# Row gathers with a growing lead, and batch 0's gathers back set among the last of them, in a routed-expert and linear-attention kernel

## The reference

```
x = x + 0.5 * ffn(layernorm(x))         # first expert stage
x = x + attn(layernorm(x))              # attention, then lookup network
x = x + 0.5 * ffn(layernorm(x))         # second expert stage

ffn(x):  probs = softmax(x @ router_W + router_b);  top1 = argmax(probs)
         h = relu(x @ W1[e] + b1[e])    # 128 -> 512, for each expert e
         y = h @ W2[e] + b2[e]          # 512 -> 128
         out = y of the expert top1, times its probability
attn(x): h = layernorm(x, g1, b1);  q, k, v = h @ wq, h @ wk, h @ wv;  16 heads of 8
         phi = elu + 1;  out = (phi(q) @ (phi(k)^T v)) / (phi(q) @ sum phi(k)) @ wo
         x = x + out;  x = x + table(layernorm(x, g2, b2) @ w1) @ w2
```

## Time and profile before

| | us |
|---|---|
| median of 3 runs | 212.8 (212.19 to 212.83) |
| profiled execution | 214.1 |
| its span | 212.4 |
| PE busy | 189.6 (89%) |
| DVE busy | 121.5 (57%) |
| POOL busy | 121.6 (57%) |
| ACT busy | 112.4 (53%) |
| mean granted TensorE clock | 0.947 of full |

### The profile page before, as it was taken

How to read it: one execution, slowest core, us unless ns; L and a number is a source line. 1 busy time by engine, 2 the same in 40 slices (tenths; PEclk the granted TensorE clock), 3 DMA queues, 4 the chain that set the end, 5 groups by cost and what they waited for, 6 DMA issues and landing times.

```text
span 212.4 us, 4556 instructions
## 1 busy us (share of the span) xinstructions
PE 189.6 (89%) x1416; PEld 159.7 (75%) x1416; DVE 121.5 (57%) x516; ACT 112.4 (53%) x328; POOL 121.6 (57%) x183
## 2 busy tenths in 40 slices
PE   4987969999997399889999999998997899999992
PEld 2963349999996398767876578688643899999991
DVE  4868312222221547889897946757531677777762
ACT  2666026555664066779869875131300766667670
POOL 6887664554467725653499704557673154455544
PEclk9965599999999679999999999999999999999998
DMA  6999959899683212059997000001028838776700
GB/s 182 256 380 346 327 166 325 266 273 305 195 297 98 73 39 77 26 204 415 420 415 315 3 2 3 27 27 44 27 74 274 279 127 296 237 258 220 260 27 0
DMA packets 26680, 40.26 MB, mean 190 GB/s; under 512 B 4229, under 2 KB 16296, under 8 KB 25632
## 3 DMA queue, kind: packets, MB, share of 16 engines
q1 hardware_dynamic: 21136, 33.01, 44.3%
q0 software_dynamic: 2496, 4.76, 7.4%
q10 hardware_dynamic: 3024, 2.20, 3.4%
HBM read 10.78 MB, written 14.46 MB: 119 GB/s over the span
## 4 chain that ended last, share of the span: by engine, by line
PE 61%; DVE 13%; issue 8%; POOL 7%; DMA 5%; ACT 4%; another core or an unknown queue 1%; POOLq 0%; DVEq 0%
PE bank L1076 19%; PE bank L1093 18%; PE bank L1213 6%; PE bank L1229 5%; PE bank L1069 2%; DMA xn_scratch<-xn 2%; DMA Xg<-xn_scratch,srcu 2%; DVE stat L1298 2%; ACT hT L726 2%; POOL xn L571 1%; PE bank L1168 1%; PE bank L1154 1%; PE bank L1178 1%; DVE phiq L1568 1%; DVE x L1531 1%
## 5 line engine op out<-in xcount | busy, mean ns | idle before, releaser
L726 ACT ACTIVATE hT<-bank,ewc_own 128x128 f32<-128x128 f32 x184 | 52.5, 368 | 50.1 <-PE bank L1076 48.7
L1076 PE MATMUL bank<-xT,ewc_own 128*128 128x128 f32 x368 | 50.3, 281 | 7.5 <-issue 5.6
L1076 PEld LDWEIGHTS bank<-xT,ewc_own 128*128 128x128 f32 x368 | 46.1, 197 | 8.7 <-issue 8.7
L1093 PE MATMUL bank<-ew,hT 128*128 x368 | 49.8, 279 | 0.5 <-ACT hT L726 0.5
L1093 PEld LDWEIGHTS bank<-ew,hT 128*128 128x128 f32 x368 | 45.6, 195 | 1.1 <-issue 1.1
L661 POOL DMA_INDIRECT out_dram<-ysb,eqrq x23 | 22.6, 983 | 26.6 <-issue 16.4
L594 POOL DMA_INDIRECT Xg<-xn_scratch,srcu x23 | 22.0, 957 | 19.2 <-PE bank L1069 15.7
L907 PE MATMUL bank<-ones_bf 128*128 128x512 bf16 x72 | 23.0, 455 | 3.1 <-POOL ident L489 2.7
L1435 DVE TENSOR_TENSOR ysb<-bank,ewc_own 128x128 f32<-128x128 f32 x23 | 6.7, 291 | 30.0 <-PE bank L1093 28.6
L653 POOL DMA_INDIRECT row_scratch<-pay,posu x16 | 15.8, 987 | 10.8 <-DVE posu L1402 6.8
L614 POOL DMA_INDIRECT xnT<-slot_scratch,posu x16 | 15.8, 988 | 10.3 <-DVE ysb L1435 4.6
(11 more groups left out here) (241 smaller groups left out, 302.2 us busy)
## 6 DMA issues: line engine op xcount, KB each, us to landing
ewc_own<-ew SPq DMA_DIRECT2D x46, 322.0 KB
row_scratch<-xn SPq DMA_DIRECT2D x8, 1024.0 KB, 10.6
ew<-in_L_ffn_W_dram SPq DMA_DIRECT2D x1, 2048.0 KB, 12.2
slot_scratch<-ysb SPq DMA_DIRECT2D x23, 64.0 KB
ew<-in_L_ffn_W_dram SPq DMA_DIRECT2D x5, 256.0 KB
eqrq<-row_scratch SPq DMA_DIRECT2D x18, 70.0 KB, 2.1
x<-in_L_attn_x_dram SPq DMA_DIRECT2D x4, 256.0 KB, 3.4
xn_scratch<-xn ACTq DMA_DIRECT2D x4, 256.0 KB, 5.8
```

Of the source, the lines that this page charges most:

```text
L726: last = A(hT[:, t.slot, c * P:(c + 1) * P], up_bank(k, c)[:, c * P:(c + 1) * P], ACT.Relu, scale=0.5 if m else 1.0, bias=ewc[t.ahead][:, ...
L1076: last = mm(up_bank(k, c)[:, c * P:(c + 1) * P], ewc[t.ahead][:, c * P:(c + 1) * P], xT[:, t.slot, :], start=True, stop=True)
L1093: last = mm(bank[4 + t.parity][:, 0:D], hT[:, t.slot, c * P:(c + 1) * P], ew[:, bass.ds(e[k], 1), W2_AT + c * D:W2_AT + (c + 1) * D].squee ...
```

## The change

`GATHERED = 4` stays the number of gathers that wait for nothing. After them the lead of the gathers over the transposes grows by one in every `GATHER_STEP = 3` gathers, up to the ring's 8 buffers (`turned_before`). From gather 21 on (`BACK_AMONG`) each gather has one of batch 0's gathers back ahead of it; the other two of batch 0 follow. The fill now stands behind the gathers back of batch 1.

```
-GATHERED = 4
+GATHERED, GATHER_STEP, BACK_AMONG = 4, 3, 21
...
+            def turned_before(k):
+
+                return k + 1 - min(UNROLL, GATHERED + (k - GATHERED) // GATHER_STEP)
+
             def move_rows():
 
                 def gather(k):
                     if k >= GATHERED:
-                        pool.wait_ge(xg_T, k - GATHERED + 1)
+                        pool.wait_ge(xg_T, turned_before(k))
...
                 for k in range(NT):
+                    if k == BACK_AMONG:
+                        pool.wait_ge(posu_ready, 1)
+                    if k >= BACK_AMONG:
+                        bring_back(0, k - BACK_AMONG)
                     gather(k)
-                g.memset(xn[:, :, :], 1.0).then_inc(fill_ready, 1)
-                pool.wait_ge(posu_ready, 1)
...
+            def bring_back(group, j):
+
+                t = group * GT + j
+                if j == 0:
+                    pool.wait_ge(y_stored[group], 16 * tiles_of(group))
+                if group + 1 < NG:
+                    pool.wait_ge(y_ready, min(NT - 1, UPTO[group] + 1 + j))
+                g.indirect_dma_start(out=Yg[:, t, :], out_offset=None, in_=slot_scr[0:UPTO[group] * P, :],
+                                     in_offset=bass.IndirectOffsetOnAxis(ap=posu[:, t:t + 1], axis=0)
+                                     ).then_inc(yb_in[group], 16)
...
             move_rows()
             for b in range(B):
-                bring_back(b)
+                for j in range(NT - BACK_AMONG if b == 0 else 0, GT):
+                    bring_back(b, j)
+                if b == 1:
+                    g.memset(xn[:, :, :], 1.0).then_inc(fill_ready, 1)
```

## The result

The changed kernel took 210.3 us, the median of 12 runs (208.67 to 212.06); the kernel before beside it took 212.91 (212.18 to 214.49, 12 runs). The ratio is 0.9873, 95% interval 0.9845 to 0.9901: faster by 2.7 us, where 6.0 were forecast and 206.8 us was the predicted time. It lies outside the range of 205.5 to 209.0.

What follows compares the result with a forecast made beforehand. PE's 5.26 us stall, from DVE's wait for batch 0's gathers back, was taken as the bound. Last down 6.4 us earlier, less 0.4 for the landing, gave 212.8 - 6.0 = 206.8 us; 8-in-10 range 205.5 to 209.0.

Steps and rivals of the forecast that it cites:

- What bounds the kernel: First expert stage: PE stalls 5.26 us before up(20), as DVE waits for batch 0's gathers back; slow matmuls follow.
- Lead of the row gathers: POOL's row gathers pull ahead, gather 20 going at about 50.7 instead of 58.2; cost and gain by itself 0.
- no wait for rows: PE did not wait for gathered rows before 67.4, busy 32.4 of 32.4 us, so the lead alone gives nothing.
- First gather back at 57.5: POOL starts batch 0's first gather back at 57.5, once the store of tile 10, issued at 54.70, has landed.
- rival A: Batch 0's data still come late: 208.8 us with the store landing late, 211.1 with back 3 late too; chance 0.12.
- Back 3 lands 2.52 us after its start on a quiet DMA: Batch 0's fourth gather back, started at 63.7, lands at 66.5 with 0.3 us added, leaving PE a 0.5 us hole.
- The fill beside DVE: The moved fill runs beside take_back and finish_rstd; POOL gives way and DVE loses at most 0.2 us.
- The sum: Last down 6.4 us earlier, less 0.4 lost to the landing: 6.0 us gained, 206.8 us forecast.
- The rest of the chain: Batch 0's statistics, guess at 69.60, normal1(0) at 71.1, then 3.84 us to the last down at 74.9, 6.4 earlier.
- B: The fill blocks DVE at the shared port during batch 0's statistics, taking 1.82 us of the gain: 208.6 us, chance 0.06.
- C: Slower: gathers 21 and 22 stand in POOL's list behind the wait for tile 10's store; 214.8 us, chance 0.03.
- D: Nothing changes, PE's hole at 67.44 having another reason than DVE's wait: 212.8 us, chance 0.04.

Runs made afterwards that it cites:

- r1: The changed kernel run again without an edit: 209.06 us beside 212.16 for the kernel before, ratio 0.9778.
- r3: The changed kernel run again without an edit, a third time: 209.8 us beside 212.97 for the kernel before, ratio 0.9885.
- r2: The changed kernel run again without an edit, a second time: 210.77 us beside 213.09 for the kernel before, ratio 0.9878.
- (2): The changed kernel with the row gathers' lead kept at 4: 0.9932 of the kernel before on a faster chip, 1.0013 and 1.0042 on slower ones.
- (4): The changed kernel with row gathers 21 and 22, then the fill, ahead of all gathers back: 206.55 of 212.16 us, 0.9726; slower chip 0.9957.
- (5): The kernel before with only the fill moved behind batch 1's gathers back: 212.52 of 212.16 us, 0.998.
- (6): The changed kernel with the fill cut into eight memsets at the same place: 209.94 of 213.09 us, 0.985; slower chip 1.0248.
- (7): (4) with ten attention weight loads moved from SP's turns 8 to 17 into its last five: 207.04 of 212.16 us, 0.9752.
- (8): (4) with weight loads of tiles 19 to 22 cut to a quarter of their columns: 206.0 of 213.09 us, 0.9668; slower chip 0.9997.
- (1): The changed kernel with the fill ahead of the wait for batch 0's first gather back: 220.26 of 216.92 us on a slower chip, 1.0127.

## Why the prediction was wrong

The steps compare best when each trace is measured from its own moment at which DVE has finished take_y(17) (start of take_back less its wait); that takes out how early or late the kernel's front ran. Us, faster chips only; "issue" is the fourth gather back's start after that moment (minus: before it), "landing" from its start to take_back, "rest" from that moment to the start of the last down:

| | issue | landing | DVE's wait | avar | rest |
|---|---|---|---|---|---|
| before; again | 2.9; 2.9 | 2.5; 2.5 | 5.5; 5.4 | 0.40; 0.17 | 15.6; 15.4 |
| forecast | -2.1 | 2.8 | 0.7 | 0.2 | 9.5 |
| changed, first trace | -0.5 | 4.3 | 3.7 | 1.70 | 15.0 |
| changed, r1; r3 | -1.7; -2.1 | 4.2; 4.4 | 2.5; 2.4 | 1.70 | 12.4; 12.4 |
| changed, r2 | -0.8 | 3.7 | 2.9 | 1.69 | 14.2 |
| (2) lead 4 | 0.0 | 2.6 | 2.5 | 2.21 | 13.0 |
| (4) rows first, fill in gap | -2.7 | 5.0 | 2.4 | 0.17 | 10.9 |
| (5) fill moved alone | 1.3 | 2.5 | 3.8 | 2.25 | 14.3 |
| (6) fill in pieces | -0.9 | 4.6 | 3.7 | 1.97 | 13.9 |
| (7) SP on time | -4.6 | 6.7 | 2.0 | 0.17 | 10.5 |
| (8) small last weights | -3.2 | at most 3.2 | 0 | 0.17 | 9.0 |

Step by step:

*What bounds the kernel* was right: PE's hole of 5.26 us shrank when the gathers back came earlier, to 3.51, 2.25, 2.71 and 2.14 in the four traces.

*Lead of the row gathers* and *no wait for rows*: gather 20 at 50.66 was forecast for 50.7, and PE stayed busy for all of 35 to 67.4 us. The cost of 0 that I took for the lead is not settled: its gain over a lead of 4 is 0.9885 against 0.9932 with overlapping intervals on one faster chip, and on the slower chips the kernels with the growing lead have the holes.

*First gather back at 57.5*: 58.98 in the first trace, where SP issued the store of tile 10 at 56.50 in place of 54.70, behind other loads and stores on its list; the landing took 2.48. Counted from the moment of the table, it was 1.5 us late there, 0.3 in r1, 1.2 in r2, and on time in r3: inside rival A. What an earlier start alone would have given, no run shows.

***Back 3 lands 2.52 us after its start on a quiet DMA ... so I go by the quiet row and add 0.3*: this step failed.** It took 3.7 to 4.4 in the four traces, between the quiet row and the busy row of 4.88 that I had set aside, and mostly nearer the busy one. I called the DMA quiet behind 64 us by the kernel before, whose share there is low:

```profile
64.00:66.00 2.00, 2.00 (x20) 2.00 (x20) 0.36 (x2) 1.15 (x4) 1.74 (x2) 1.00 0.34 104
```

But it is the changed kernel's traffic that counts, with the gathers back now in the time of the last tiles' weights, the stores and the row gathers: 1.00 in the first trace, 0.97 in r1, 0.81 in r2, 0.75 in r3. The table suggests how little an earlier issue is worth there: from (2) over r3 to (4) it goes from 0.0 to -2.7, and DVE's wait only from 2.5 to 2.4. (8) takes the load of the last weights away, and the wait goes; that this load is what makes the landing late rests on this one trace. The share does not tell the whole: in 66 to 68, around the issue, it was 0.43 in r2 and the landing 3.7 us, and 0.65 in (2) and the landing 2.6. r3 issued exactly as forecast (-2.1), so the landing alone is the error: 2.4 - 0.7 = 1.6 us by the unrounded waits.

***The fill beside DVE: POOL gives way and DVE loses at most 0.2*: this step failed too.** DVE lost 1.70 - 0.17 = 1.5 us on the chain of the changed kernel, 1.5 to 2.1 in all ten traces with the whole fill in that place, and nothing in the six where the fill stood in the gap. The nearest row I took, a combine beside POOL's arithmetic, was a SCALAR_TENSOR_TENSOR; the one that met the fill is a TENSOR_SCALAR from SBUF to SBUF. The Trainium skill, SBUF — State Buffer, "Who interferes with whom", separates the two: tensor_scalar can enter a two-port mode, in which it contends with GpSimd, while an instruction with at most one SBUF input outside such a mode does not. The trace agrees at both ends: 1.70 us for avar, 0.29 and 0.28 for the instructions that read a PSUM bank beside the fill in (4); whether avar ran in such a mode no run shows. I had cited only the general sentence on that page and dismissed it; this one tells which instruction to look for. I had also put the fill at 68.7 to 70.5, into a gap; with the gathers back late it came at 72.35, onto avar.

*The sum.* 1.6 + 1.5 = 3.1 us to be taken off 6.0 leaves 2.9. The four comparisons gave 2.6 (by medians), 3.1, 2.3 and 3.2 us. In the table, 9.5 + 3.1 = 12.6 against 12.4 in r1 and r3. The first trace and r2 have 15.0 and 14.2. Their waits are longer, 3.0 and 2.2 above the forecast, which makes 9.5 + 3.0 + 1.5 = 14.0 and 9.5 + 2.2 + 1.5 = 13.2. The 1.0 left over in each fits the down and the up that run slow on their chains (1.92 and 1.71 us, 1.80 and 1.71, for 0.89 at a clock of 1.00); no run separates it.

*The rest of the chain* (statistics, guess, four relus with normal1, last down) was right. (8), without the late landing and without the port, has 9.0, where the forecast less its 0.4 is 9.1; (1), (4) and (8) on the slower chips, where DVE does not wait and the fill is in the gap, have 8.6. (4) has the late landing alone: 9.5 + 1.6 = 11.1, measured 10.9. Its gain in the table is 4.6 us against 5.6 by the medians; the interval of the ratio reaches from 4.6 to 7.1.

*The rivals.* A and B were both true, together; I had priced them singly, 208.8 and 208.6, with 0.12 and 0.06. Against the forecast, A's first case cost 2.0 us and its second 4.3, and DVE waited 1.6 to 3.0 longer than forecast; but A had the first gather back late, while in r3 it was on time and the landing alone was late. B's 1.8 was about right (1.5). They are not independent: data that come late carry avar into the fill. Had I worked out both at once, 206.8 + 1.6 + 1.5 = 209.9 would have been on the page. C did not happen on the faster chips: in the first trace gather 21 went at 60.23, and PE had no hole in front of turn(21). D is out.

## What to carry to other kernels

A transfer moved earlier is moved into another traffic: read the DMA share where it will travel, after the change, and take the loaded landing unless the transfer leaves behind the last of that traffic. When a fill on POOL is moved, list every DVE instruction it can now meet, and look for an SBUF-to-SBUF TENSOR_SCALAR among them, however small: here it stood until the fill had ended, and cutting the fill up didn't help; a place beside DVE instructions that read a PSUM bank did. Two rivals that make each other likelier need a price together.

## What the runs showed of the hardware

- The fourth gather back, 64 KB, took 2.5 to 2.6 us to land in the four traces (faster chips) that issued it at 67.0 or later, and 3.7 to 6.7 in the seven with whole weights that issued it earlier.
- A TENSOR_SCALAR over 128x4 took 1.69 to 2.25 us beside a memset of 1.82 on POOL, and 1.97 beside eight of together 2.09.
- The same code differs by chip: 212.2 to 213.1 us on one kind and 216.6 to 216.9 on another, and edit (4), which gains 5.6 us on the first, gains at most 2 on the second.
- The same code differs by execution: the two traces of the kernel before have spans of 212.4 and 209.9, and the four of the changed kernel 210.3, 209.3, 211.3 and 208.1.
